# Two attention layers and two feed-forward layers on one core: FP4's shift on VectorE a step later, and the run-ins of FP4 and of the first tile in another order

## What is computed

```python
x = x + cross_attention(layernorm(x), ctx, L0_xattn_*)        # 16 heads of 16, softmax over 77 keys
x = x + quantum_ffn(layernorm(x), L0_ffn_*)                   # 256 -> 1024 -> 256, sine in the hidden layer
x = x + cross_attention(layernorm(x), ctx, mask, L1_xattn_*)  # the same, with a key mask
h = layernorm(x)
gate, up = fp4_linear(h, w_gate), fp4_linear(h, w_up)         # 256 -> 704
x = x + fp4_linear(silu(gate) * up, w_down)                   # 704 -> 256
```

## Time and profile before

| | us |
|---|---|
| median of 3 runs (lowest to highest) | 926.62 (925.99 to 928.49) |
| the profiled execution, its own time | 927.38 |
| its span, first to last instruction | 925.6 |
| TensorE matmuls busy in it | 885.8 (96%) |
| VectorE busy | 779.7 (84%) |
| ScalarE busy | 522.2 (56%) |
| GpSimd busy | 459.8 (50%) |
| mean granted TensorE clock | 0.993 |

### The profile page before, as it was taken

The page is one execution under the profiler, slowest core; times in us unless marked ns, Lnnn a source line. Parts: engine busy times, 40 slices in busy tenths (PEclk is TensorE's granted clock), DMA queues, the critical chain, the costliest instruction groups (busy, mean ns, idle before and its releaser), DMA issues.

```text
span 925.6 us, 20182 instructions
## 1 busy us (share of the span) xinstructions
PE 885.8 (96%) x7216; PEld 797.3 (86%) x7216; DVE 779.7 (84%) x2117; ACT 522.2 (56%) x1147; POOL 459.8 (50%) x661
## 2 busy tenths in 40 slices
PE   7899999999899999999899999998879999999998
PEld 5799999998799999988899999997758888888886
DVE  6999999999677777755999999997868898989886
ACT  3534343434688888886665656564644544444443
POOL 2233433342566677745224333432247777777772
PEclk9999999999999999999999999998989999999999
DMA  9120000000000000001000000000000000000001
GB/s 328 72 104 2 2 2 1 2 2 1 2 1 1 1 1 2 1 1 56 1 2 2 1 2 2 2 2 1 1 1 1 24 24 24 1 24 23 24 1 46
DMA packets 6515, 18.31 MB, mean 20 GB/s; under 512 B 912, under 2 KB 3344, under 8 KB 5904
## 3 DMA queue, kind: packets, MB, share of 16 engines
q1 hardware_dynamic: 5552, 16.65, 4.7%
q10 hardware_dynamic: 864, 0.37, 0.2%
HBM read 12.83 MB, written 4.19 MB: 18 GB/s over the span
## 4 chain that ended last, share of the span: by engine, by line
PE 70%; DVE 10%; ACT 9%; POOL 6%; issue 3%; DMA 1%; ACTq 0%; POOLq 0%; DVEq 0%
PE a_psO L1230 14%; PE s_psY L1448 10%; PE s_psH L1437 9%; PE f_psGU L1941 7%; PE a_psQ L1192 6%; PE a_psT L1219 6%; PE a_psS L1171 5%; PE f_psY L1933 5%; ACT a_qTs L1116 3%; ACT a_prob L1099 3%; POOL f_hval L1772 2%; PE a_psQ L1180 2%; POOL f_hres L1778 2%; PE a_psY L1180 1%; DVE f_hid L1609 1%
## 5 line engine op out<-in xcount | busy, mean ns | idle before, releaser
L1230 PE MATMUL a_psO<-vblk,a_prob 128*128 128x51 f32 (+1 forms) x1280 | 148.4, 271 | 0.0
L1230 PEld LDWEIGHTS a_psO<-vblk,a_prob 128*128 128x128 f32 x1280 | 148.0, 192 | 0.0
L1941 PE MATMUL f_psGU<-late_wgu,f_xTs 128*128 128x512 f32 (+1 forms) x576 | 141.4, 390 | 6.3 <-ACT late_wdT L1874 3.2
L950 DVE TENSOR_REDUCE a_mx<-a_psS 128x4 f32<-128x308 f32 x256 | 115.2, 471 | 9.2 <-PE a_psS L1171 3.9
L1941 PEld LDWEIGHTS f_psGU<-late_wgu,f_xTs 128*128 128x128 f32 x576 | 104.0, 192 | 21.2 <-ACT late_wdT L1874 3.4
L1099 ACT ACTIVATE a_prob<-a_psT 128x512 f32<-128x512 f32 (+1 forms) x192 | 101.8, 530 | 23.7 <-PE a_psT L1219 22.6
L958 DVE TENSOR_TENSOR a_shifted<-a_psS,a_mx 128x308 f32<-128x308 f32 x256 | 114.8, 469 | 0.0
L1219 PE MATMUL a_psT<-ident,a_shifted 128*128 128x128 f32 x640 | 106.2, 281 | 8.3 <-ACT a_prob L1099 5.0
L1087 ACT COPY a_xTs<-a_psQ 128x256 f32<-128x256 f32 x64 | 23.9, 373 | 159.8 <-PE a_psQ L1180 159.6
L1448 PEld LDWEIGHTS s_psY<-e_w,s_hid 128*128 128x128 f32 x768 | 100.1, 188 | 8.7 <-POOL s_hid L1368 3.5
L1368 POOL TENSOR_TENSOR s_hid<-s_full,s_hid 128x512 fp32r<-128x512 f32 x64 | 82.9, 1296 | 45.8 <-ACT s_full L1403 45.8
(11 more groups left out here) (193 smaller groups left out, 1830.3 us busy)
## 6 DMA issues: line engine op xcount, KB each, us to landing
out_x<-x SPq DMA_DIRECT2D x7, 512.0 KB, 2.6
x<-in_x SPq DMA_DIRECT2D x3, 1024.0 KB, 16.0
w<-in_w SPq DMA_DIRECT2D x1, 2304.0 KB, 8.7
w<-in_w SPq DMA_DIRECT2D x2, 1024.0 KB, 13.8
a_mask<-in_mask SPq DMA_DIRECT2D x4, 308.0 KB, 3.8
wat<-in_att SPq DMA_DIRECT2D x1, 1024.0 KB, 15.2
x<-in_x SPq DMA_DIRECT2D x1, 768.0 KB, 10.5
wat<-in_att SPq DMA_DIRECT2D x2, 256.0 KB, 4.9
```

The lines of the kernel that those rows point to most:

```text
L950: nc.vector.tensor_reduce(mx[:, u, j * BH:(j + 1) * BH], psS[j][:, 0:BH * KV].rearrange("p (h k) -> p h k", k=KV), AX.X, ALU.max).then_inc ...
L1230: mm = nc.tensor.matmul(psO[:, CH[c] * VW:(CH[c] + n) * VW], prob[:, u, c * P:(c + 1) * P], vblk[:, t // R, c * NJ * VW:(c * NJ + n) * VW] ...
L1941: mm = nc.tensor.matmul(psGU[:, n0:n1], xTs[:, u, a, k * P:(k + 1) * P], wgu[:, b, k, n0:n1], start=(n == 0), stop=(n == len(TERMS) - 1))
```

## The change

VectorE's `shifts` moves from the end of FP4 step i (i % 4 == 2) to the beginning of step i + 1. In FP4's run-in ScalarE copies the last three weight groups inside step -2, ahead of `x_high(0)`, and loads the table and makes the high part of tile 31 in another order; VectorE makes tile 31's low part ahead of its step -1, and TensorE projects tile 31 ahead of FP4's step 0. In the program's first tile VectorE takes the statistics of tiles 1 and 2 and the normalisation of tile 1 later, and TensorE computes both halves of the values behind the first scores.

```diff
@@ VectorE, first tile @@
                 att0.keys.key_low(dve, 0)
-                a.sums(1, 1)
-                a.moments(1)
                 att0.keys.key_low(dve, 1)
                 dve.wait_ge(g["pairmask_set"], 1)
                 att0.keys.first_keys_on_vector(dve)
                 a.query_low(0, 0)
-                a.normalise(1, 1)
-                a.sums(2, 0)
-                a.moments(0)
+                a.sums(1, 1)
+                a.moments(1)
                 for i in range(0, T):
                     a.step_scores(i, i % 2)
                     if i == 0:
+                        a.sums(2, 0)
+                        a.moments(0)
                         dve.wait_ge(inputs.in_const, 16 * 2)
                         att0.keys.bias_row(dve)
@@ VectorE, FP4's run-in @@
                 f4.step(-2, a.outputs)
+                a.output_low(T - 1, 1)
                 f4.step(-1)
-                a.output_low(T - 1, 1)
                 a.residual(T - 1)
@@ ScalarE, FP4's run-in @@
-                f4.step(-2)
+                f4.step(-2, range(fp4.LOWS, len(fp4.groups)))
+                a.attended_high(T - 1, 1)
                 inputs.table(act, ACT.Silu)
-                for n in range(fp4.LOWS, len(fp4.groups)):
-                    f4.weight_copy(n)
-                a.attended_high(T - 1, 1)
                 f4.step(-1)
@@ TensorE, first tile @@
-                pe.wait_ge(inputs.in_w0, 16)
-                att0.keys.value_product(pe, 0)
                 for i in range(0, T):
                     a.scores(i, i % 2)
                     if i == 0:
-                        att0.keys.value_product(pe, 1)
+                        pe.wait_ge(inputs.in_w0, 16)
+                        att0.keys.value_products(pe)
@@ TensorE, FP4's run-in @@
                 f4.step(-1)
                 a.attended(T - 1, 1)
+                a.projected(T - 1, 1)
                 f4.step(0)
-                a.projected(T - 1, 1)
@@ Keys: new, calls value_product for both halves @@
+    def value_products(self, pe):
+        for h in range(KC):
+            self.value_product(pe, h)
@@ Attention.vector, step_scores @@
             row_max(i, u, 0)
+            if l == 0 and i == 0:
+                normalise(1, 1)
             row_max(i, u, 1)
@@ Fp4.vector, step @@
+            if i % SG == 3 and valid(i + 5):
+                shifts((i + 5) // SG)
             if valid(i):
                 hidden(i, i % 2)
...
-            if i % SG == 2 and valid(i + 6):
-                shifts((i + 6) // SG)
@@ Fp4.scalar, step @@
-        def step(i):
+        def step(i, copies=()):
...
                 normalise(i + 5, (i + 5) % 2)
+            for n in copies:
+                weight_copy(n)
             if valid(i + 2):
                 x_high(i + 2, i % 2)
```

## The result

The changed kernel took 923.0 us (median of 8 runs, 917.53 to 924.33), the kernel before 927.58 us in the same comparison. The ratio is 0.9939, with a 95% interval of 0.9924 to 0.9953: a small gain of 0.6%, clear of the noise. The forecast was 916.8 us, in a range of 914.8 to 919.8. The sign was right; the size was not: the gain is about 5.7 us where 9.8 were forecast, and the measured median lies outside the range.

A forecast was written before the change was run, and what follows sets the result against it. TensorE, busy 96% of the span, was taken as the bound, with single long waits to remove. The terms -5.8 - 3.6 - 0.4 = -9.8 us took the median 926.62 to 916.8 us, range 914.8 to 919.8.

The forecast's parts named there:

- Part 1: FP4's first shift, in attention 1: moved a step later, VectorE no longer waits for GpSimd's power; -5.8 us.
- part 2: FP4's run-in: first product starts earlier, at full clock, and `hidden(0)` follows sooner; -0.9 - 1.85 - 0.85 = -3.6 us.
- the slower rival: FP4's loop settles in a worse phase, with 0.45 us more a step; time 930 us, chance 0.02.
- the renamed wait: FP4's run-in: late `attended_high` holds up the first product, leaving only 0.7 us of gain there; 919.7 us, chance 0.08.
- part 3: First tile: scores begin earlier but the values' first half runs behind them; -0.4 us, bounds -1.6 and +0.3.
- the clock in the sum: FP4's run-in: half clock behind the old 3.2 us gap costs 1.85 us, saved as the 1.6 us gap keeps full clock.
- the clock's fall in the new gap at FP4's run-in: Rival: the clock falls in the new 1.6 us gap, leaving 1.75 us of gain there; 918.7 us, chance 0.15.
- My bound of +0.3: First tile: worst case +0.3 us, if a VectorE operation in front of the maxima turns out to be the last.

The follow-up runs named there:

- e4: Kernel before with only the first tile's new order; 930.44 us (median of 12), ratio 1.0022.
- e15: Kernel before with only the first tile's new order, run again; 931.06 us (median of 12), ratio 1.0021.
- e2: Kernel before with only FP4's shift a step later on VectorE; 921.11 us (median of 6), ratio 0.9925.
- e11: Kernel before again, no edit, for its trace; 926.15 us at a mean clock of 0.994.
- e3: Kernel before with only FP4's run-in in its new order; 926.10 us (median of 12), ratio 0.9981.
- e5: Changed kernel with the first tile in its old order; 919.59 us (median of 6), ratio 0.9919 of before.
- e10: Changed kernel with the first tile in its old order, run again; 918.73 us (median of 6), ratio 0.9911 of before.
- e16: Changed kernel with the first tile in its old order, a third time; 921.17 us (median of 6), ratio 0.9909 of before.
- e6: Changed kernel plus five matmuls of zeros on TensorE ahead of the first scores; 919.30 us (median of 6), ratio 0.9924 of before.
- e7: Changed kernel with the values' first half back ahead of the first scores on TensorE; 920.26 us (median of 6), ratio 0.9919 of before.
- e13: Changed kernel with the first tile's old order, plus five filler matmuls in TensorE's wait for `silu(1)` in FP4; 920.98 us.
- e8: Changed kernel again, no edit, for its trace; one execution, 922.54 us at a clock of 0.991.
- e9: Changed kernel again, no edit; 921.27 us (median of 6), ratio 0.9934 of before.
- e12: Changed kernel with the first tile's old order, plus nine filler matmuls in TensorE's wait for `silu(1)` in FP4; 919.53 us (median of 6).
- e1: Changed kernel again, no edit; 919.98 us (median of 6), ratio 0.9919 of before.

## Why the prediction was wrong

**Right.** Part 1: its place, its cover (`normalise(0)` waits 0.5 us, `input_copy(31)` is not late), and its size: 5.86 us in the trace, 6.6 on the averages. The mechanism of part 2: the idle time ahead of `projected(31)` is 1.6 us, the clock stays up in it in every trace with the new run-in, and `hidden(0)` follows the products. The loop of FP4 is untouched, so the slower rival as I put it did not come; nor did the renamed wait. In part 3, the 0.4 us of the chain.

**Wrong: the sum's basis.** The step that failed is the clock in the sum ("So the half clock costs 1.85 us there" and "-1.85"): it took the clock of one execution of before as the kernel's, and 1.00 in the changed parts as the changed kernel's. In *part 2*, 1.85 us of the 3.6 were the clock behind the 3.2 us gap. It is low there in some executions with the old run-in and not in others (low in the first profile, e4 and e15, up in e2 and e11), where the sum books it whole. The term as measured is 1.5 us on the average (e3, 0.2 to 2.7) where 3.6 were forecast; the clock explains a part of the difference, and the rest is open.

**Wrong: part 3.** "-0.4" was mis-sized and has the wrong sign on the average: +2.3 us alone (e4, e15), +1.7 us in the whole change (against e5, e10 and e16). I counted where the values' first half went and not what it had done where it was: it kept TensorE busy between its queries and the first scores. I looked for the clock's fall in the new gap at FP4's run-in, made it a rival, and put the clock at nothing in the gap of 1.4 us that part 3 opens. My bound of +0.3 for this part did not hold the cost. That the cost goes mostly with a lower clock is measured; that this gap is what lowers it is not shown.

With the three measured terms, -6.6 - 1.5 + 2.0 (between 1.7 and 2.3) = -6.1 us, the sum is where the result is (-5.7 by the ratio, -6.5 by all averages).

**A slip in a rival.** The renamed wait needed ScalarE to be 2.2 us late. By the prediction's own times, 672.2 against 673.1, 0.9 us is enough to bring the first product back to where it was. It did not matter here.

**Open.** That the first tile's new order costs time, with a lower mean clock, is measured twice. By what it lowers the clock, and where in the complete change, is not settled: the two traces of the order alone show 12 to 19 us, while four traces of the complete change don't, and two of these show 31, 235 and 457 us, places that e16 has with the old order too. That the new order lets the attention begin at a moment that depends on how the first matmuls ran (its first scores came at 11.40 to 13.73 us in four traces), where the old one mostly waits for a transfer (12.58 to 12.96 in six traces of nine with that order), may be why such executions are more frequent; this is argued, not shown. The transfer that TensorE waits for ahead of tile 0 is the other candidate, above all for the falls in the first tile. Whether filling the idle time (e6, e7) cures it is open too.

The version without part 3 (e5, e10, e16) averages 919.84 us over 18 executions: 0.88% below before, and 1.7 us below the changed kernel. Only e7, with the values' first half back, averages a little less (919.63), over six.

## What to carry to other kernels

One profiled execution shows what a change does to the chain, but not what the clock does on the average: where a term of a sum is TensorE's half level, look at further executions before it is booked, and ask of each new idle time, also of one far off the stage in question, what stood in it before. A wait that is removed gains what the next wait leaves: e13 gave TensorE its full clock and 1.5 us, and the next wait took all of it. A wait for a neighbour's result at the end of a step (the shift) can be cured by taking the consumer a step later, if the engine's queue has a margin there. And when two versions' traces differ in where the clock falls, compare first what they do ahead of the changed lines.

## What the runs showed of the hardware

The granted clock's half level came, in one and the same program, at different places from one execution to the next: 31, 235 and 457 us in e7, e8, e9 and e16, one or two places near these in e3, e12 and e15, none of them in the eleven other traces. Executions of the changed kernel lay up to 8.1 us apart (917.53 to 925.66). A busy TensorE is no guard: in e16 it was busy from 27.4 to 38 us without a gap, after an idle time of 0.8 us, and at 29.8 us it fell to the half level all the same. Nor does an idle time have to bring the clock down: TensorE waited 3.2 us in FP4's run-in in e2 and e11, and 2.7 and 2.9 us in FP4's first steps in e3, and the clock stayed at 1.00.

At the beginning of the program the matmuls run slow while the profile's clock still reads 1.00: key products of 850 ns beside such of 422 ns in the first profile after. The Trainium skill (TensorE: Matmul & The Clock Gate, Part 1) says that such a start varies from run to run of one kernel; the traces here agree (the key products took 2.31 us in all in e5 and 4.13 in e1), and show the same for falls in the middle of a program.
